# A gated two-block transformer layer pair: VectorE and ScalarE take the steps of the token stage in another order

## What is computed

```python
x = x + tanh(g_xattn[0]) * L0_xattn(ctx, layernorm(x), conv_w, conv_b)   # rows of a memory: shifted x, a small convolution, ctx
x = x + tanh(g_ffn[0])   * L0_ffn(layernorm(x), weight, bias)            # layernorm, rounded to fp6 blocks of 32, times a rounded weight
x = x + tanh(g_xattn[1]) * L1_xattn(layernorm(x), ctx, mask, U_w, D)     # relu keys, softmax over 77 context rows
x = x + tanh(g_ffn[1])   * L1_ffn(layernorm(x), Wr, W1, W2)              # router to 1 of 8 experts, capacity 1280, two products
```

## Time and profile before

| what | value |
|---|---|
| median of 3 runs | 2230.97 us (2230.48 to 2230.99) |
| the profiled execution | 2233.29 us, its span 2231.6 us |
| mean granted TensorE clock | 0.943 of full speed |
| busy in the span: TensorE, VectorE, ScalarE, GpSimd | 89%, 45%, 37%, 30% |
| token stage (0 to 912 us): VectorE busy / TensorE busy, 480 to 766 us of it | 219 us / 239 us of 286 |
| experts' stage (912 us to the end): TensorE busy | 1284 us of 1319 |

### The profile page before, as it was taken

How to read it: one execution, slowest core, us unless ns; L and a number is a source line. 1 busy time by engine, 2 the same in 40 slices (tenths; PEclk the granted TensorE clock), 3 DMA queues, 4 the chain that set the end, 5 groups by cost and what they waited for, 6 DMA issues and landing times.

```text
span 2231.6 us, 35225 instructions
## 1 busy us (share of the span) xinstructions
PE 1981.0 (89%) x11276; PEld 1712.4 (77%) x11277; DVE 1011.4 (45%) x2286; ACT 830.3 (37%) x1805; POOL 671.5 (30%) x579
## 2 busy tenths in 40 slices
PE   4469788888788897399999999999999999999997
PEld 2457676677676675288888999899889899889986
DVE  3667777777777764615142123212513323312241
ACT  2234656565656654514142113211422312311241
POOL 0434333334333321315152114311522412311250
PEclk9579889999989997699999999999999999999999
DMA  6221223333233332715142003300421502401130
GB/s 187 89 82 33 101 95 131 119 120 115 105 108 110 132 134 95 232 39 160 61 141 93 28 28 113 108 28 28 154 78 47 169 28 66 137 28 38 47 116 16
DMA packets 152258, 208.66 MB, mean 94 GB/s; under 512 B 12830, under 2 KB 78622, under 8 KB 152197
## 3 DMA queue, kind: packets, MB, share of 16 engines
q1 hardware_dynamic: 111125, 114.14, 16.3%
q0 software_dynamic: 15728, 43.38, 6.3%
q10 hardware_dynamic: 25344, 50.33, 6.0%
HBM read 140.98 MB, written 68.37 MB: 94 GB/s over the span
## 4 chain that ended last, share of the span: by engine, by line
PE 57%; ACT 0%; issue 0%; DMA 0%; POOL 0%; POOLq 0%; DVEq 0%; ACTq 0%; DVE 0%
PE bank L1737 23%; PE bank L1745 22%; PE bank L1710 5%; PE bank L1690 5%; PE bank L1668 1%; PE bank L1699 1%; DMA tg<-t_d,idx_t 0%; PE bank L1674 0%; ACT w_hi L1601 0%; ACT w_hi L1602 0%; POOLq L1442 0%; DMA slots<-slot_d 0%; POOL out_dram L1480 0%; DVEq L1383 0%; ACT inT_hi L1587 0%
## 5 line engine op out<-in xcount | busy, mean ns | idle before, releaser
L1828 DVE SCALAR_TENSOR_TENSOR hT_lo<-bank,hT_hi 128x256 fp32r<-128x256 f32 x352 | 149.3, 424 | 656.9 <-ACT hT_hi L1632 643.1
L1632 ACT ACTIVATE hT_hi<-bank 128x256 fp32r<-128x256 f32 x352 | 135.1, 384 | 748.0 <-PE bank L1737 746.9
L1737 PE MATMUL bank<-inT_hi,w_lo 128*128 128x256 f32 x1408 | 398.5, 283 | 0.0
L1737 PE MATMUL bank<-inT_lo,w_hi 128*128 128x256 f32 x1408 | 398.3, 283 | 0.0
L1737 PE MATMUL bank<-inT_hi,w_hi 128*128 128x256 f32 x1408 | 396.8, 282 | 0.0
L1745 PE MATMUL bank<-w_hi,hT_hi 128*128 128x512 f32 x704 | 279.9, 398 | 0.0
L1737 PEld LDWEIGHTS bank<-inT_hi,w_hi 128*128 128x128 f32 x1408 | 269.0, 191 | 13.4
L1737 PEld LDWEIGHTS bank<-inT_lo,w_hi 128*128 128x128 f32 x1408 | 269.0, 191 | 12.0
L1745 PE MATMUL bank<-w_lo,hT_hi 128*128 128x512 f32 x704 | 277.7, 394 | 0.0
L1745 PE MATMUL bank<-w_hi,hT_lo 128*128 128x512 f32 x704 | 274.1, 389 | 0.0
L1737 PEld LDWEIGHTS bank<-inT_hi,w_lo 128*128 128x128 f32 x1408 | 269.0, 191 | 0.0
(11 more groups left out here) (303 smaller groups left out, 4154.1 us busy)
## 6 DMA issues: line engine op xcount, KB each, us to landing
stage<-in_L_ffn_W_dram SPq DMA_DIRECT2D x256, 256.0 KB, 3.0
X<-in_x_dram SPq DMA_DIRECT2D x16, 1024.0 KB, 5.2
t_d<-tt ACTq DMA_DIRECT2D x16, 1024.0 KB
x_d<-x ACTq DMA_DIRECT2D x16, 1024.0 KB, 4.3
out_dram<-y ACTq DMA_DIRECT2D x16, 1024.0 KB, 4.2
xs<-in_x_dram SPq DMA_DIRECT2D x16, 768.0 KB
cw_a<-in_L_xattn_conv_w_dram SPq DMA_DIRECT2D x2, 1024.0 KB, 17.5
cw_b<-in_L_xattn_conv_w_dram SPq DMA_DIRECT2D x2, 1024.0 KB, 19.6
```

What stands on the lines that cost most here:

```text
L1632: act.activation(hT_hi[:, f % 4, :], hb[f % 4][:, 0:CN], ACT.Relu).then_inc(e_hh, 1)
L1737: last = pe.matmul(hb[f % 4][:, 0:CN], l[:, k, fs], r[:, k, :], start=(n == 0), stop=(n == 3 * KB - 1))
L1828: dve.scalar_tensor_tensor(out=hT_lo[:, f % 4, :], in0=hb[f % 4][:, 0:CN], scalar=0.0, in1=hT_hi[:, f % 4, :].bitcast(F32), op0=ALU.max, o ...
```

## The change

VectorE: the routing of group d (from `lb` to `counts`) is now ahead of z's moments; it was behind z's `nb_a`. The two means are no longer made by VectorE: ScalarE makes them, each directly in front of its squares (`squares` got the row sum as an argument; semaphores `a_mc` and `a_md` take the place of `v_nm` and `v_nd`). The group e's `rsc`, `nb_d`, `y_sc`, `y_nb` go from the start of the step to behind `scf`, and `rsum`, `rp` and the slots go from ahead of add_linear(1) to behind add_attention(0). Kind b's moments go ahead of add_linear(1), `shift("b")` behind it.

ScalarE: `re_`, `tt` and its store go from the start of the step to behind group a's normalised `n1`, so that `tt`, two stores and `y` now stand side by side ahead of `up(0)`. The high parts of `n1` 0 and 1 go ahead of the normalisation of `xs`, those of 2 and 3 behind `up(3)`, which itself stands behind the normalisation. The squares of `x3` and `rs_d` go from behind `up(2)` to the end of the step, behind `sT`. TensorE's, GpSimd's and SyncE's lists stay as they were.

```diff
-            def squares(x, g, nm, sq, s, told, spare):
+            def squares(x, g, total, nm, sq, s, added, told, spare):
+
+                wait(act, added, T * (g + 1))
+                act.activation(nm[:, :], total[:, :], ACT.Copy, scale=-1.0 / D).then_inc(told, 1)
                 wait(act, told, g + 1)
...
@@ ScalarE's body
-                if d is not None:
-                    squares(lambda j: x3[:, ds((d % 2) * T + j, 1), :], d, nm_d, sq_d, a_sd, v_nd, junk_d)
                 if z is not None:
                     rstd("a", z)
-                up(3)
-                if d is not None:
-                    rstd_of_squares("d", d, sq_d, a_sd, rs_d[:, :])
+                quantised_hi(0)
+                quantised_hi(1)
                 if z is not None:
...
-                for j in range(T):
-                    quantised_hi(j)
+                up(3)
+                quantised_hi(2)
+                quantised_hi(3)
                 for j in range(T):
                     second_hi(j)
...
+                if d is not None:
+                    squares(lambda j: x3[:, ds((d % 2) * T + j, 1), :], d, sum_d, nm_d, sq_d, a_sd, v_x3, a_md, junk_d)
+                    rstd_of_squares("d", d, sq_d, a_sd, rs_d[:, :])
@@ VectorE's body
-                    dve.tensor_scalar(nm_d[:, :], sum_d[:, :], -1.0 / D, None, ALU.mult).then_inc(v_nd, 1)
-                if z is not None:
-                    wait(dve, s_xs, 48 * (z + 1))
-                    moments("a", z, lambda j: xs[:, j, :])
-                up_rest(2)
...
                     dve.tensor_tensor(counts[:, :], counts[:, :], ohs[:, :], ALU.add).then_inc(v_oh, 1)
+                if z is not None:
+                    wait(dve, s_xs, 48 * (z + 1))
+                    moments("a", z, lambda j: xs[:, j, :])
+                up_rest(2)
```

More of the change, by code:

```diff
@@ L653, in body @@
                 if e is not None:
+                    wait(act, v_re, 3 * e + 1)
+                    act.activation(re_[:, :, :], rsc[:, :, :], ACT.Exp).then_inc(a_re, 1)
+                    wait(act, v_ys, 3 * e + 1)
+                    wait(act, s_t, 16 * e)
+                    settled(act)
+                    for j in range(T):
+                        act.activation(tt[:, j, :], x3[:, ds(xe + j, 1), :], ACT.Identity, bias=nb_d[:, j:j + 1],
+                                       scale=rs_d[:, j:j + 1]).then_inc(a_tt, 1)
+                    wait(act, a_tt, T * (e + 1))
+                    act.dma_start(t_d[ds(er, G), :].rearrange("(j p) e -> p j e", p=P), tt[:, :, :]).then_inc(s_t, 16)
                     if d is not None:
@@ L1092, in body @@
                                              op0=ALU.mult, op1=ALU.mult).then_inc(v_sm, 1)
-                if e is not None:
-                    wait(dve, a_re, e + 1)
-                    dve.tensor_reduce(rsum[:, :], re_[:, :, :], AX.X, ALU.add).then_inc(v_re, 1)
-                    wait(dve, v_re, 3 * e + 2)
-                    dve.reciprocal(rp[:, :], rsum[:, :]).then_inc(v_re, 1)
-                    slots_of(e)
-                add_linear(1)
                 if a is not None:
@@ L1102, in body @@
                     moments("b", a, lambda j: tile_of(a, j))
+                add_linear(1)
+                if a is not None:
+                    shift("b", a)
                 if d is not None:
@@ L1109, in body @@
                     dve.tensor_scalar(scf[:, :], srd[:, :], gx[:, ds(d, 1)], None, ALU.mult).then_inc(v_scf, 1)
+                if e is not None:
+                    wait(dve, a_rs["d"], 2 * (e + 1))
+                    wait(dve, v_r, 8 * e + 5)
+                    dve.tensor_tensor(rsc[:, :, :], rd[:, :, :], per_expert(rs_d), ALU.mult).then_inc(v_re, 1)
+                    wait(dve, a_md, e + 1)
+                    dve.tensor_tensor(nb_d[:, :], nm_d[:, :], rs_d[:, :], ALU.mult).then_inc(v_ys, 1)
+                    dve.tensor_scalar(y_sc[:, :], rs_d[:, :], gates[:, 3:4], 1.0, ALU.mult, ALU.add).then_inc(v_ys, 1)
+                    wait(dve, v_ys, 3 * e + 1)
+                    dve.tensor_scalar(y_nb[:, :], nb_d[:, :], gates[:, 3:4], None, ALU.mult).then_inc(v_ys, 1)
                 add_linear(2)
-                if a is not None:
-                    shift("b", a)
                 add_attention(0)
+                if e is not None:
+                    wait(dve, a_re, e + 1)
+                    dve.tensor_reduce(rsum[:, :], re_[:, :, :], AX.X, ALU.add).then_inc(v_re, 1)
+                    wait(dve, v_re, 3 * e + 2)
+                    dve.reciprocal(rp[:, :], rsum[:, :]).then_inc(v_re, 1)
+                    slots_of(e)
                 add_linear(3)
-                if b is not None:
-                    wait(dve, v_x2, T * (b + 1))
-                    wait(dve, a_sq, T * b)
-                    dve.tensor_scalar(nm_c[:, :], sum_c[:, :], -1.0 / D, None, ALU.mult).then_inc(v_nm, 1)
                 add_attention(1)
```

56 lines of the change are left out of this document (16 added, 40 removed).

## The result

| | before | after |
|---|---|---|
| median | 2230.98 us (2230.48 to 2236.19, 4 runs) | 2198.05 us (2197.48 to 2198.33, 4 runs) |
| ratio, 95% interval | | 0.9847 (0.9830 to 0.9864) |
| span of the profiled execution | 2231.6 us | 2195.8 us |
| mean granted TensorE clock | 0.943 | 0.946 |
| busy in the span: TensorE, VectorE, ScalarE, GpSimd | 89%, 45%, 37%, 30% | 90%, 46%, 38%, 30% |

The change makes the kernel 1.5% faster. The forecast was 2186 in a range of 2172 to 2206: the time lies in the range, and the gain is 33 us where 45 were expected. Steps are numbered t = 0 to 20 by the newest group; the loop is t = 6 to 15. The step of after that is shown opens at 455.00 and ends at 501.5.

The account below looks back on a forecast made before the run. The prediction took TensorE's 6.9 us wait per step for xdT_lo of row 0 to bound the token stage. Its terms, 28.5+5.5+9.9+3.2-2 = 45.1 us, taken from 2231.0, gave 2186 us, range 2172 to 2206.

Parts of the forecast that it names:

- The bound: In each token-stage step, TensorE's transposes of n1 wait 6.9 us for VectorE's xdT_lo; nothing else of size shortens a step.
- Part 1: On VectorE, nm_d's 3.69 us goes, but lb<-lb,scf then stands until GpSimd's gbias ends, so the stall only changes its name.
- Rival 3: On VectorE, the multiplication lb does not stand behind gbias; moments 1.4 us earlier or more, 2169 us; chance 0.04.
- Part 2: From the end of gbias to TensorE's release: 6.95 us instead of 8.83, a gain of 1.9 us.
- Part 3: GpSimd's gbias ends 0.7 us earlier (bounds 1.1 and -1.0), so TensorE is released 2.55 us earlier per step.
- rival 1: ScalarE is late through its stores, or half clock lasts longer; gain 1.2 us a step, 26 us, 2205; chance 0.14.
- Part 4: Behind TensorE's release: the shorter pause lets the clock give back 0.3 us a step; up_hi(3) behind the normalisations costs nothing.
- the cover of 0.6 us: Margin at TensorE's last turn of X: up_lo(3) comes at 519.4, needed at 520.1 at the present pace.
- The sum: Ten steps 28.5, two before them 5.5, three early steps 9.9, last step with group a 3.2, drain -2: 45.1 us.
- 2: Larger gain: most steps keep TensorE's upper clock and gbias ends 1.1 us earlier; 56 us, 2175; chance 0.13.
- 5: No change: routing and ScalarE take what z gains, the early steps' gain goes to the drain; 2228 to 2234; chance 0.03.
- 4: Slower: ScalarE's row ahead of up_hi(0) becomes the bound, 5 us late in all; +15 us, 2246; chance 0.05.

Follow-up runs that it names:

- short_bias: The changed kernel with GpSimd's addition X<-X,gbias cut to 8 of the 512 columns, the other 504 left without bias; 2157.81 us.
- z_first: The changed kernel with VectorE's routing behind nb_a again, so z's moments come first behind the last add_attention; 2139.92 us.
- stores_behind_y: The changed kernel with ScalarE's stores of t_d and x3_d issued behind y and up(0) instead of between tt and y; 2181.65 us.
- up3_first: The changed kernel with up_hi(3) ahead of the normalisation of xs on ScalarE instead of behind it; 2196.61 us.
- up3_busy: up3_first with 20 extra products, results unread, in TensorE's pause behind project(3); 2174.17 us.
- hi_behind_xs: The changed kernel with the high parts of n1 0 and 1 behind the four normalisations of xs again; 2253.55 us.
- together: The changed kernel with z's moments first, routing behind up_lo(3), up_hi(3) ahead of xs's normalisation, two stores behind y; 2123.68 us.
- together_places: together with TensorE's five small products that count places moved from ahead of the scores to behind them; 2112.75 us.
- busy_pause: The changed kernel with 20 extra products, results unread, in TensorE's pause behind project(3) wherever groups a and d exist; 2192.24 us.
- before_means: The kernel before with the two means made by ScalarE in front of its squares, every order kept; 2224.97 us.

## Why the prediction was right, and where it was short

- **The bound** (TensorE waits for `xdT_lo` of row 0, and nothing else of size): right. Every kernel's step followed its release, except where `up_lo(3)`, the clock or the places came in behind it.
- **Part 1, the lock goes on under the name of lb**: right, 4.29 us ending with gbias; short_bias shows it by taking gbias away. Rival 3 is refuted.
- **Part 2, gbias to release 6.95 us**: measured 492.76-485.72 = 7.04, against 8.83 before and 6.95 forecast: right. What the step did not ask is what could run *inside* gbias. z_first shows that z's moments can, and that the order which the change chose costs 60 us against that one.
- **Part 3, gbias ends 0.7 us earlier**: this is the term that failed. It ended 0.15 earlier (sT+30.72 against 30.87), and with it the release came 1.95 us earlier a step, not 2.55. I had up_hi(0) at sT+18.3; it came at 18.83, because `n1` began at sT+8.84 instead of 8.4 (VectorE's `nb_b` now stands behind add_linear(1), 463.41) and because the two stores took 1.27 us, not the 1.13 of the earlier trace rows. The prediction wanted `up_hi(0)` at most 0.2 us behind what TensorE gives; project(0) ends at 472.3 and `up_hi(0)` starts at 473.83, 1.5 us behind it. stores_behind_y shows the chain by taking 1.39 off up_hi(0) and 0.85 off the release. The first half of rival 1, ScalarE late, was thus the truth in a mild form; the 2.31 us of one store in the loop's first step were in neither, and left that step a gain of only 0.46 us.
- **Part 4, the clock gives 0.3 back, up_hi(3) costs nothing**: the first half is wrong, the second right for this kernel alone. From the release to the next sT come 8.04 us on average, 8.13 before. In after the lower clock comes in each step, but in some from sT+34 to 41 and in others from 37 to 44 (once to 40.5), so the turns of X take 2.3 to 3.2 us from the first start to the last. up3_first shows that up_hi(3) costs nothing as long as this is so. But the cover of 0.6 us holds only at half clock: VectorE's up_lo(3) shows 2.38 us of wait, and up3_busy shows that at 1.00 it costs 1.3 us a step.
- **The sum**: ten loop steps 18.6 us, not 28.5; t=4 and 5 5.3 (5.5); ahead of the first sT 11.5 (9.9), which hi_behind_xs confirms as the high parts' own gain; t=16 2.2 (3.2); the drain -1.8 net (-2): 35.8 for 45.1. That the drain fits is luck. `al` does come 0.9 us later in each of the two steps, as forecast; but steps 17 and 18 gain 2.0 us all the same, and the tail loses 3.8, since slots and scatters stand too late there, which the prediction had held to be free. The rest of the 12 us between forecast and median is that the profiled execution before lay 2.3 us over its median, so that 2.3 us of the spans' difference are no gain of the medians, and that of after (2197.48) lay 0.6 under.
- **Rivals**: 2 and 5 did not come; 4 (ScalarE's first half becomes the bound) has its mechanism confirmed and its price refuted, 0.55 us late and not 5.

## What to carry to other kernels

When one engine's long instruction locks another out, taking the first stalled operation away only names the next one; ask of every operation in the queue whether it can run beside the lock, and put those that can there. Here those were the `bn_stats`, which read one tensor from SBUF; the tensor_scalar `nm_d` reads one as well and could not (3.69 us). A move's worth is the distance to the next thing in the queue, so the same edit was worth 24 us in one kernel and 55 in the other. Two costs that cover each other each look free when removed alone.

## What the runs showed of the hardware that was not expected

- Hundredths of a microsecond in start decide 4.4 us. In together and together_places, `counts` took 0.17 us in all 20 steps in which it began 0.12 to 0.19 us ahead of GpSimd's addition, and 4.55 to 4.60 us in the four in which it began 0.01 to 0.04 us behind. The Trainium skill, "SBUF — State Buffer", section "Who interferes with whom", says that the issue order decides who blocks; these rows agree.
- The same store costs ScalarE's queue 0.39 us in a steady step and 2.31 us in the first pass of the loop. It did so in five more kernels that have the store ahead of `y` (2.10 to 2.52 us), but not in busy_pause and up3_busy; the traces do not tell why.
- TensorE's clock fell in stretches in which the engine had hardly paused: in busy_pause in t=11 and t=16, in up3_busy in t=11. Windows of busy_pause (stretch; us; busy by engine; clock; DMA; GB/s), each time 28 us with over 27.8 busy and the 3 us behind them:

```profile
493.00:521.00 28.00, 27.81 (x144) 22.38 (x142) 22.85 (x63) 21.38 (x52) 10.87 (x9) 1.00 0.46 162
521.20:524.20 3.00, 3.00 (x8) 2.32 (x9) 2.88 (x5) 0.00 (x0) 3.00 (x2) 0.50 0.21 52
...
718.30:746.30 28.00, 27.87 (x151) 22.76 (x149) 23.16 (x63) 21.83 (x53) 11.69 (x9) 1.00 0.43 151
746.30:749.50 3.20, 3.20 (x11) 2.52 (x10) 3.09 (x4) 0.00 (x0) 3.20 (x2) 0.50 0.03 5
```

  In t=11 it put the turns of `n1` 0 and 1 back by 1.55 us, of which the wait behind them took up all but 0.2. In before_means the same came in three of the ten loop steps (in t=9 behind 27.9 us with 26.9 busy) and cost 1.5 us each. What made the clock fall there is open.
